# Three queues reordered: centring the first batch's weights later in each step, and a new order of DVE's and ACT's work behind attention

## Chip, cores and metric

The kernel runs on one core of one Trainium2 chip. The metric is the device time of one launch in microseconds (us). PE is TensorE (matmuls and transposes), DVE is VectorE, ACT is ScalarE, POOL is GpSimd, and SP is SyncE, which here only issues transfers. Each engine has a queue of its own, works it off in order, and waits at semaphores.

## What is computed

Eight sequences of 256 tokens, width 256, go through a gated attention layer and a gated mixture of experts:

```python
x = x + tanh(g_xattn) * attention(layernorm(x), ctx)     # self (256 keys) and cross (64 keys)
x = x + tanh(g_ffn) * moe(layernorm(x))                  # 8 experts, 2 for each token, one shared expert

# attention: ln -> fp8 rounding -> q, qx (16 heads), k, v (8 groups), each q and k head with a
# layernorm of its own over its 128 columns; kx, vx from ctx in full precision; softmax; p @ v;
# both outputs divided by a smoothing vector, rounded to fp8, and projected by wproj
```

## The kernel before

**Attention** runs in steps n = 0 to 63: step n = 8b + g belongs to batch b and head group g. A step is a software pipeline. In step n, PE projects q, k, v of group n, transposes the normalised heads of group n-1, scores group n-1, multiplies the probabilities of group n-4 by v, and projects group n-5 out. The first batch is written out step by step (`tick(0, g)`); the other seven run in a loop. Steps 64 to 68 drain the pipeline and already hold work of the experts.

**What each engine does in a step, in its queue's order.** ACT: `copy_q` (the projected q to SBUF, L884), `square_q`, in the first batch `scale(k)`, then squares and copies of k, `high_p`, `key_maps` (L913), `exp_cross`, `high_v`, and last `exp_self` (L924). DVE: `read_q` twice (L1236), the sums of squares (`squares_q`, which waits for ACT's `square_q` of the same step), variances (L1250), `low_p` (L1208), the row maxima of the scores (L1203, which wait for PE, which waits for `key_maps`), `low_v` (L1219), `copy_x` (L1230), reciprocals, and the next batch's front: statistics in steps 0 and 1, `front_scale` in step 2, a clip in step 3. POOL: the roots (L1693), the product that normalises q (L1760), k (L1767, waits for `copy_x`), `probx` (L1737) and `prob` (L1744), and in steps 0 and 1 the next batch's layernorm (L1697, L1700).

**The weights of the first batch.** The projections' weights come in eight pieces, k = 0 to 7, one for each group, through two staging buffers. For each piece DVE sums the heads (`sum_heads`, L1150), turns the sums to means (`head_means`) and subtracts them from the scaled weights (`centre`, eight instructions, L1166); ACT rounds the result to f16 (`high(k)`, L832); and POOL takes the rest (`prepare(k)` on POOL, `w_lo`, L1727). Piece 0 is made before step 0, pieces 1 and 2 in step 0, and piece k in step k-2 after that. PE may project step k when `w_lo` of piece k is there. SP loads piece k into its buffer when `w_lo` of piece k-2 is done. The transposing transfer `flip(0)`, which brings the probabilities of group 0 to where PE multiplies them by v in step 4, stands in SP's queue behind the wait for `w_lo` of piece 5.

In DVE's step the parts of one piece lie apart: `sum_heads` between the two `read_q`, `centre` in the middle, ahead of the maxima. On ACT, `high(k)` stands ahead of `exp_self`.

**Behind attention.** The experts' weights are split into an f16 high part (ACT, `ffn_high(u)`, L837) and a low part (DVE, `ffn_low(u)`, L1180), in units u = 0 to 4: u = 0 is the shared expert, the others hold two experts each. The shared expert runs for six pieces m = 0 to 5 in the first half: PE `shared_up(m)`, ACT `shared_silu(m)`, DVE `shared_mul(m)` (L1584), ACT `shared_high(m)` (L850), POOL `shared_low(m)` (L1810), PE `shared_down(m)` (L659 to L661). DVE adds its results to x in `finish(q)` (L1595). Routing is DVE's: `ranks`, `count_tiles`, `plan_tiles`, `read_table`, `read_tokens` (the row addresses, `f_idx`), `slots` and `mix_weights`. POOL then gathers the experts' rows with indirect transfers (`fetch_z(j)`, L1820), behind `tail_low` of the last batch (L1721), which waits for ACT's `tail_high` (L818). The experts' loop of 39 tiles begins on PE with `expert_up(0)`, which waits for all five `ffn_low`; PE's `turn_z(1)` waits for `finish(3)`; DVE's `expert_mul(0)` follows `mix_weights`.

Of the kernel before, what the change touches and what calls it, by code (L numbers as in the profile page):

```python
# [16 lines left out]
B, S, SC, H = 8, 256, 64, 256  # L17
# [57 lines left out]
def build(nc, x, wallT, wpT, w13T, w2e, s1T, s3T, s2, gateT, ctxT, vecs, scal, ident, rconst, rtri, out):  # L75
    ctx = ExitStack()
    with ctx:
# [725 lines left out]
        def _(act):  # L803
# [11 lines left out]
            def tail_high(tb):  # L815
                done(act, ta_z, tb)
                act.wait_ge(zr_read, tb * 32 + 16)
                nc.scalar.activation(zr[:, :, 0, :], zf[:, :, :], ACT.Copy).then_inc(ta_hi, 1)  # L818
# [33 lines left out]
            def tick(b, g):  # L852
# [162 lines left out]
                    front_scale(b + 1)  # L1015
                if g == TAIL_G and live(b - 1, B):
                    tail_high(b - 1)
                for k in preps[-1:]:
                    high(k)
                for h in range(HPG):  # L1020
                    if live(n0 - 1): exp_self(n0 - 1, par(1), h)

            act.wait_ge(ld_vec, 48)
            nc.scalar.activation(gates[:, 0:2], scl[:, S_GX:S_GF + 1], ACT.Tanh).then_inc(tanh_done, 1)
# [44 lines left out]
            ffn_high(3)  # L1069
            shared_silu(3)  # L1070
            ffn_high(4)
            shared_high(3)
            shared_silu(4)
            tail_high(B - 1)
            shared_high(4)
            shared_silu(5)
            shared_high(5)
# [13 lines left out]
        def _(dve):  # L1091
# [98 lines left out]
            def tick(b, g):  # L1190
# [91 lines left out]
                if isinstance(n0, int) and n0 >= STEPS:  # L1282
                    if g == 0:
                        for k in (1, 0): read_q(n0 - 1, par(1), k)
                        whole_out(n0 - 5, par(5))
                        maxima(n0 - 2, par(2), 2)
                        low_p(n0 - 3, par(3))
                        low_px(n0 - 3, par(3))
                        for k in range(2): maxima(n0 - 1, par(1), k)
                        sums(n0 - 2, par(2))  # L1290
                        read_logits(0, 0, NE, A1)
                        done(dve, mm_kT, STEPS - 1)
                        best(0, 0, NE, 0)
                        maxima(n0 - 1, par(1), 2)
                        best(0, 0, NE, 1)
                        members(0, NE)
                        sums(n0 - 1, par(1))
                        low_p(n0 - 2, par(2))
                        low_px(n0 - 2, par(2))
                    if g == 1:  # L1300
                        ranks(0)
                        count_tiles(0)
                        whole_out(n0 - 5, par(5))
                        low_p(n0 - 2, par(2))
                        low_px(n0 - 2, par(2))
                        ffn_low(0)
                    if g == 2:
                        whole_out(n0 - 5, par(5))
                        for t in range(4): marks(t)
                        ffn_low(1)  # L1310
                        shared_mul(0)
                    if g == 3:
                        whole_out(n0 - 5, par(5))
                        for t in range(4, 8): marks(t)
                        shared_mul(1)
                        whole_out(n0 - 4, par(4))
                        for t in range(8, NE): marks(t)
                        shared_mul(2)
                    return
# [2 lines left out]
                    prepare(k)  # L1322
                if tail and g == LAGS: residual(b - 1)
                if live(n0 - 1): read_q(n0 - 1, par(1), 1)
                if preps and n0 > 0: sum_heads(preps[-1])
                if live(n0 - 1): read_q(n0 - 1, par(1), 0)
                if live(n0): squares_q(n0, par(0))
                if live(n0): low_vx(n0)
# [3 lines left out]
                if live(n0 - 2): maxima(n0 - 2, par(2), 2)  # L1332
                if live(n0 - 5): round_out(n0 - 5, par(5))
                if live(n0): variances_k(n0, par(0))
                if preps and n0 == 0:
                    low_v(n0)
                    copy_x(n0, par(0))
                    sum_heads(preps[-1])
                if preps: head_means(preps[-1])
                for c in range(HC if preps else 0): centre(preps[-1], c)  # L1340
                if live(n0 - 3): low_p(n0 - 3, par(3))
                if live(n0 - 3): low_px(n0 - 3, par(3))
                if between and g == G - 1:
                    done(dve, mm_q1, n0)
                    front_round(b + 1, 0)
                if live(n0 - 1): maxima(n0 - 1, par(1), 0)
                if live(n0) and not (preps and n0 == 0):
                    low_v(n0)
                    copy_x(n0, par(0))
                if live(n0 - 1): maxima(n0 - 1, par(1), 1)  # L1350
                if live(n0 - 2): sums(n0 - 2, par(2))
                if between:
                    if isinstance(n0, int) and n0 == 0:
                        dve.wait_ge(ld_x, 16)
                    if g == 0: front1(b + 1)
                    if g == 1: front2_stats(b + 1)
                    if g == FRONT_G: front_scale(b + 1)
                    if g == FRONT_G + 1: front_clip(b + 1)
                    if g == G - 1:
                        done(dve, mm_kv, n0)  # L1360
                        front_round(b + 1, 2)
                if tail:
                    if g == LAGS: tail1(b - 1)

# [271 lines left out]
            tail1(B - 1)  # L1636
            plan_tiles(0)
            read_table(0)
            ffn_low(2)
            read_tokens(0)  # L1640
            for q in range(2): finish(q)
            shared_mul(3)
            ffn_low(3)
            shared_mul(4)
            ffn_low(4)
            shared_mul(5)
            slots(0)
            for q in range(2, 4): finish(q)
            mix_weights(0, 0, NE)
# [244 lines left out]
```

## Time and profile before

| | |
|---|---|
| median of 3 runs | 967.53 us (966.03 to 969.52) |
| the profiled execution's own time | 960.57 us |
| its span in the trace | 958.8 us |
| busy, share of the span | PE 86%, DVE 83%, ACT 79%, POOL 76% |
| first batch's steps 1 to 6 | about 48 to 135 us |
| loop of batches 1 to 7 | to about 720 us |
| first tile of the experts' loop | at 796.66 us |

A row of the timeline gives start and duration in us, engine, line, operation, output <- inputs with their shapes, and in brackets the engine's idle time before it and who ended it.

### The profile page before, as it was taken

Reading aid. Unit: us, or ns where it says so; the run is one execution under the profiler, and the core shown is the slowest. Engines: PE = TensorE matmul, PEld = TensorE weight load, DVE = VectorE, ACT = ScalarE, POOL = GpSimd, SP = SyncE. Lnnn points to the kernel's source line nnn. Section 1 sums busy time; section 2 is a strip of 40 time slices with the busy share of each in tenths; the row PEclk is TensorE's granted clock in tenths of the full one; section 3 lists DMA queues with packets and bytes.
Section 4 is the critical chain, followed back from the end, with each engine's and each line's share of the span. In section 5 each row is a group of like instructions: output and inputs, shape, how many; then the busy total and the mean of one; then the engine's idle time right before and its main releaser. Section 6 shows DMA issues by size and latency. Waiting matters only on the chain.

```text
span 958.8 us, 21329 instructions
## 1 busy us (share of the span) xinstructions
PE 825.3 (86%) x6498; PEld 638.5 (67%) x6498; DVE 799.0 (83%) x1857; ACT 756.2 (79%) x2392; POOL 725.2 (76%) x570
## 2 busy tenths in 40 slices
PE   0467699999999999999999999999995858888396
PEld 0345478788778778878777877877874436666254
DVE  7999889998998998999898899989888986743148
ACT  3367799999999999999999999999997433444132
POOL 4398689899889989988998998899896145444633
PEclk9777999999999999999999999999999799999689
DMA  9521433235234324324324333333337524556433
GB/s 247 130 88 45 100 66 74 57 60 101 55 58 85 70 55 82 77 55 82 77 55 78 59 77 72 64 77 75 61 85 173 147 88 111 131 140 145 125 120 112
DMA packets 213837, 87.64 MB, mean 91 GB/s; under 512 B 190080, under 2 KB 207456, under 8 KB 213792
## 3 DMA queue, kind: packets, MB, share of 16 engines
q1 hardware_dynamic: 205936, 74.76, 34.9%
q0 software_dynamic: 7856, 12.33, 5.9%
q8 instruction: 23, 0.38, 0.2%
q14 instruction: 22, 0.18, 0.1%
HBM read 31.88 MB, written 10.22 MB: 44 GB/s over the span
## 4 chain that ended last, share of the span: by engine, by line
PE 35%; POOL 23%; DVE 15%; issue 14%; ACT 7%; DMA 3%; another core or an unknown queue 2%; DVEq 0%; POOLq 0%; SPq 0%; ACTq 0%
POOL rstd L1693 8%; POOL raw L1760 5%; PE A L432 5%; PE A L433 5%; PE T L498 4%; PE S L527 3%; POOL prob L1744 3%; PE S L515 2%; DVE stage L1166 2%; DVE ss L1241 2%; POOL z L1700 2%; DMA psrc<-w_lo 2%; POOL z L1697 2%; ACT zq L811 2%
## 5 line engine op out<-in xcount | busy, mean ns | idle before, releaser
L1693 POOL TENSOR_TENSOR rstd<-var,mhalf 128x8 f32<-128x8 f32 (+1 forms) x128 | 190.3, 1503 | 54.3 <-DVE var L1250 53.9
L432 PE MATMUL A<-w_hi,xq 128*128 128x256 f16 (+1 forms) x1024 | 190.2, 251 | 36.6 <-DVE v_lo L1219 20.7
L433 PE MATMUL A<-w_lo,xq 128*128 128x256 f16 (+1 forms) x1024 | 190.4, 252 | 0.0
L1236 DVE TENSOR_SCALAR qT<-T,qmap 128x512 f32<-128x512 f32 x128 | 103.5, 810 | 56.8 <-PE T L498 56.5
L527 PE MATMUL S<-kT,qT 128*128 128x256 f32 x512 | 139.1, 395 | 5.6 <-ACT kT L913 4.9
L432 PEld LDWEIGHTS A<-w_hi,xq 128*128 128x128 f16 x1024 | 102.0, 100 | 49.0 <-issue 32.2
L924 ACT ACTIVATE prob<-S,nmx 128x256 f32<-128x256 f32 x256 | 122.0, 503 | 7.1 <-DVE nmx L1203 5.2
L527 PEld LDWEIGHTS S<-kT,qT 128*128 128x128 f32 x512 | 92.8, 191 | 45.8 <-ACT kT L913 27.9
L1760 POOL TENSOR_TENSOR raw<-raw,rstd 128x1024 f32<-128x1024 f32 x64 | 121.2, 1894 | 0.0
L1744 POOL TENSOR_TENSOR prob<-prob,rl 128x1024 f32<-128x1024 f32 x64 | 121.0, 1891 | 0.0
L1203 DVE TENSOR_REDUCE nmx<-S 128x2 f32<-128x512 f32 (+1 forms) x192 | 113.5, 591 | 4.1 <-PE S L527 3.4
L433 PEld LDWEIGHTS A<-w_lo,xq 128*128 128x128 f16 x1024 | 102.1, 100 | 8.2
L498 PE MATMUL T<-idt,raw 128*128 128x128 f32 x512 | 82.1, 285 | 8.4 <-POOL raw L1760 7.4
L1820 POOL DMA_INDIRECT w_lo<-zd,w_lo x46 | 45.2, 982 | 54.1 <-PE VB L747 26.7
L884 ACT ACTIVATE raw<-A 128x512 f32<-128x512 f32 x128 | 81.5, 637 | 4.5 <-PE A L433 4.5
L932 ACT ACTIVATE probx<-S,nmx 128x64 f32<-128x64 f32 x256 | 78.0, 338 | 3.7 <-DVE nmx L1203 3.6
L1208 DVE SCALAR_TENSOR_TENSOR psrc<-prob,psrc 128x1024 f16<-128x1024 f32 x64 | 78.3, 1224 | 1.6 <-ACT psrc L948 1.5
L1241 DVE TENSOR_REDUCE ss<-sq 128x8 f32<-128x1024 f32 x64 | 77.4, 1209 | 0.0
L877 ACT ACTIVATE sq<-A 128x512 f32<-128x512 f32 x128 | 72.4, 639 | 4.0 <-PE A L433 4.0
L498 PEld LDWEIGHTS T<-idt,raw 128*128 128x128 f32 x512 | 61.4, 146 | 18.1 <-POOL raw L1760 15.7
L557 PE MATMUL JB<-wp,yb 128*128 128x256 f16 x512 | 67.2, 275 | 6.3 <-DVE yb L1271 6.3
L948 ACT ACTIVATE psrc<-prob 128x1024 f16<-128x1024 f32 x64 | 67.9, 1061 | 1.4 <-POOL prob L1744 1.4
(257 smaller groups left out, 2434.1 us busy)
## 6 DMA issues: line engine op xcount, KB each, us to landing
stage<-wallT SPq DMA_DIRECT2D x8, 1024.0 KB, 5.1
yd<-pT SPq DMA_DIRECT2D x46, 128.0 KB
wp<-wpT POOLq DMA_DIRECT2D x1, 2048.0 KB, 31.0
zd<-zr SPq DMA_DIRECT2D x8, 256.0 KB, 2.4
out<-xs SPq DMA_DIRECT2D x8, 256.0 KB
xs<-x SPq DMA_DIRECT2D x1, 1792.0 KB, 21.0
raw<-w13T SPq DMA_DIRECT2D x2, 704.0 KB, 4.6
pT<-psrc SPq DMA_TRANSPOSE x64, 4.9
```

The costliest lines, as they stand in the source:

```text
L432: nc.tensor.matmul(o, l, w_hi[:, c, col:col + n], start=(c == 0), stop=False)
L433: last = nc.tensor.matmul(o, l, w_lo[:, c, col:col + n], start=False, stop=(c == HC - 1))
L498: last = nc.tensor.transpose(o[:, h * S + t * P:h * S + (t + 1) * P], raw[:, p, UQ + t * 2 * HPG + k * HPG + h, :], idt[:, :])
L527: last = nc.tensor.matmul(o[:, t * S:(t + 1) * S], qT[:, p, 0, h, t * P:(t + 1) * P], kT[:, p, 0:S], start=True, stop=True)
L884: last = nc.scalar.activation(raw[:, p, u, :], o, ACT.Copy)
L924: last = nc.scalar.activation(prob[:, p, :, j, :], o[:, t * S:(t + 1) * S].rearrange("p (k s) -> p k s", s=P), ACT.Exp, bias=nmx[:, p, j:j ...
L1203: nc.vector.tensor_reduce(nmx[:, p, j:j + rows], o[:, 0:rows * w].rearrange("p (r w) -> p r w", w=w), AX.X, ALU.max, negate=True).then_inc ...
L1236: nc.vector.tensor_scalar(qT[:, p, k, :, :].rearrange("p h s -> p (h s)"), o[:, :], qmap[:, 2 * k:2 * k + 1], qmap[:, 2 * k + 1:2 * k + 2] ...
L1241: nc.vector.tensor_reduce(ss[:, p, 0:UK], sq[:, p, 0:UK, :], AX.X, ALU.add).then_inc(d_ssq, 1)
L1693: return nc.gpsimd.tensor_tensor(dst, src, mhalf[:, 0:n], ALU.pow)
L1744: nc.gpsimd.tensor_tensor(prob[:, p, :, :, :], prob[:, p, :, :, :], rl[:, p, 0:PJ].rearrange("p (o j i) -> p o j i", o=1, i=1).to_broadcas ...
L1760: nc.gpsimd.tensor_tensor(raw[:, p, 0:UK, :], raw[:, p, 0:UK, :], rstd[:, p, 0:UK].rearrange("p (u o) -> p u o", o=1).to_broadcast([P, UK, ...
```

## The change

It has two parts. In the first batch, DVE makes a whole piece of weights (`prepare(k)`: sums, means, centring) at the end of its step, behind the maxima and the next batch's front; the special order of step 0 goes; and on ACT `high(k)` stands behind `exp_self`. Behind attention, DVE runs `ranks` and `count_tiles` behind `ffn_low(0)`; `finish(0)` and `finish(1)`, `read_tokens(0)`, `shared_mul(3)` and `shared_mul(4)` ahead of `ffn_low(2)`, and `shared_mul(5)` ahead of `ffn_low(3)`; and ACT runs `tail_high` of the last batch ahead of `shared_high(3)`. No instruction is added, removed or altered, and no buffer or wait is another.

```diff
 # ACT, end of a step
+                for h in range(HPG):
+                    if live(n0 - 1): exp_self(n0 - 1, par(1), h)
                 for k in preps[-1:]:
                     high(k)
-                for h in range(HPG):
-                    if live(n0 - 1): exp_self(n0 - 1, par(1), h)
...
 # ACT, behind step 68
             ffn_high(4)
+            tail_high(B - 1)
             shared_high(3)
             shared_silu(4)
-            tail_high(B - 1)
...
 # DVE, step 65
                     if g == 1:
-                        ranks(0)
-                        count_tiles(0)
                         whole_out(n0 - 5, par(5))
                         low_p(n0 - 2, par(2))
                         low_px(n0 - 2, par(2))
                         ffn_low(0)
+                        ranks(0)
+                        count_tiles(0)
...
 # DVE, a step of the first batch
                 if live(n0 - 1): read_q(n0 - 1, par(1), 1)
-                if preps and n0 > 0: sum_heads(preps[-1])
                 if live(n0 - 1): read_q(n0 - 1, par(1), 0)
...
-                if preps and n0 == 0:
-                    low_v(n0)
-                    copy_x(n0, par(0))
-                    sum_heads(preps[-1])
-                if preps: head_means(preps[-1])
-                for c in range(HC if preps else 0): centre(preps[-1], c)
...
                 if live(n0 - 1): maxima(n0 - 1, par(1), 0)
-                if live(n0) and not (preps and n0 == 0):
-                    low_v(n0)
-                    copy_x(n0, par(0))
+                if live(n0): low_v(n0)
+                if live(n0): copy_x(n0, par(0))
                 if live(n0 - 1): maxima(n0 - 1, par(1), 1)
...
                         front_round(b + 1, 2)
+                for k in preps[-1:]:
+                    prepare(k)
...
 # DVE, behind step 68
             read_table(0)
+            for q in range(2): finish(q)
+            read_tokens(0)
+            shared_mul(3)
+            shared_mul(4)
             ffn_low(2)
-            read_tokens(0)
-            for q in range(2): finish(q)
-            shared_mul(3)
+            shared_mul(5)
             ffn_low(3)
-            shared_mul(4)
             ffn_low(4)
-            shared_mul(5)
             slots(0)
```

## Rows read from the trace of the kernel before

**Rows 1.** Stretches: busy us of PE, PEld, DVE, ACT, POOL (instructions), granted clock, DMA.

```profile
40.00:60.00 20.00, 12.34 (x66) 8.56 (x65) 19.53 (x45) 10.32 (x25) 15.61 (x13) 0.67 0.28 101
...
220.00:300.00 80.00, 78.23 (x626) 62.92 (x624) 72.74 (x164) 78.61 (x264) 72.24 (x57) 1.00 0.36 70
```

**Rows 2.** Timeline of ACT in the first batch: `copy_q` of steps 1, 2, 5, 7.

```profile
47.56 0.58 ACT L884 ACTIVATE raw<-A 128x512 f32<-128x512 f32 x1
...
59.98 0.61 ACT L884 ACTIVATE raw<-A 128x512 f32<-128x512 f32 x1
...
71.77 1.91 ACT L832 ACTIVATE w_hi<-stage 128x2048 f16<-128x2048 f32 x1 [1.03 <-DVE stage L1166]
...
108.99 0.64 ACT L884 ACTIVATE raw<-A 128x512 f32<-128x512 f32 x1
...
113.88 0.89 ACT L913 ACTIVATE kT<-T,vec 128x256 f32<-128x256 f32 x2
...
135.30 0.61 ACT L884 ACTIVATE raw<-A 128x512 f32<-128x512 f32 x1
```

**Rows 3.** Timeline of DVE in the first batch.

```profile
60.92 1.80 DVE L1150 TENSOR_REDUCE msum<-stage 128x6 f32<-128x768 f32 x2
...
67.41 1.14 DVE L1166 SCALAR_TENSOR_TENSOR stage<-stage,vec,msum 128x256 f32<-128x256 f32 x3
...
68.67 2.81 DVE L1166 SCALAR_TENSOR_TENSOR stage<-stage,vec,msum 128x256 f32<-128x256 f32 x3
...
105.02 0.69 DVE L1203 TENSOR_REDUCE nmx<-S 128x2 f32<-128x512 f32 x1 [2.39 <-PE S L527]
```

**Rows 4.** Timeline of POOL in the first batch.

```profile
51.78 0.69 POOL L1693 TENSOR_TENSOR rs<-ve,mhalf 128x2 f32<-128x2 f32 x1
...
61.78 1.04 POOL L1700 TENSOR_TENSOR z<-z,rs 128x512 f32<-128x512 f32 x1
...
66.97 2.49 POOL L1693 TENSOR_TENSOR rstd<-var,mhalf 128x8 f32<-128x8 f32 x2
69.44 1.89 POOL L1760 TENSOR_TENSOR raw<-raw,rstd 128x1024 f32<-128x1024 f32 x1
73.00 0.83 POOL L1767 TENSOR_TENSOR raw<-raw,rstd 128x384 f32<-128x384 f32 x1 [1.68 <-DVE raw L1230]
...
74.36 1.90 POOL L1744 TENSOR_TENSOR prob<-prob,rl 128x1024 f32<-128x1024 f32 x1
```

**Rows 5.** The chain that ended last: start, us, what.

```profile
92.04 4.05 POOL w_lo L1727
...
96.11 5.01 DMA pT<-psrc
...
131.53 0.97 PE S L527 x4
```

**Rows 6.** Timeline of DVE behind attention.

```profile
756.03 0.43 DVE L1266 TENSOR_SCALAR yb<-yb 128x1024 f16<-128x1024 bf16 x1 [0.59 <-ACT yb L957]
...
775.31 2.75 DVE L1180 SCALAR_TENSOR_TENSOR w_lo<-sq,w_hi 128x1408 f16<-128x1408 f32 x2
...
789.26 0.69 DVE L1584 SCALAR_TENSOR_TENSOR zq<-S,qT 96x512 f32<-96x512 f32 x1 [2.43 <-POOL w_hi L1810]
789.87 1.79 DVE L1570 TENSOR_TENSOR ctx_hi<-ctx_hi,ctx_lo 128x192 f32<-128x192 f32 x1
...
795.52 0.88 DVE L1595 SCALAR_TENSOR_TENSOR xs<-VB,gates,xs 128x256 f32<-128x256 f32 x2 [1.51 <-issue]
```

**Rows 7.** Timeline of POOL behind attention.

```profile
782.28 1.94 POOL L1721 TENSOR_TENSOR zr<-z,zr 128x512 f16<-128x512 f32 x1 [9.20 <-ACT zr L818]
784.38 2.30 POOL L1820 DMA_INDIRECT w_lo<-zd,w_lo  x1 [0.17 <-issue]
```

**Rows 8.** Timeline of ACT behind attention.

```profile
780.57 0.63 ACT L850 ACTIVATE w_hi<-zq 128x512 f16<-128x512 f32 x1 [6.01 <-DVE zq L1584]
```

**Rows 9.** Timeline of PE: the first matmul of `expert_up(0)`.

```profile
796.66 0.32 PE L424 MATMUL S<-w_hi,psrc 128*128 x1 [0.60 <-issue]
```

## The prediction

> **What bounds the kernel now.** I read the stretches first. In the loop of batches 1 to 7 ACT is busy for 78.6 of 80 us and PE for 78.2 [rows 1]; nothing of the change lies there, and what the first batch loses or gains simply shifts the loop. In the first batch the picture is another: from 40 to 60 us DVE is busy for 19.5 of 20 us, ACT for 10.3 and PE for 12.3 [rows 1]. There DVE sets the pace. Then I read the timelines of ACT, DVE and POOL side by side, with `copy_q` as the mark of a step: step 1 takes 12.4 us (47.56 to 59.98), steps 2 to 4 take 49.0, steps 5 and 6 take 26.3 [rows 2]. The loop's step is about 10.2: 264 ACT instructions in 80 us, some 33.6 of them to a step [rows 1].
>
> Two things are to be seen in DVE's rows. Centring c = 0 takes 1.14 us, the same three instructions for c = 1 take 2.81 [rows 3], and the added 1.67 us lie inside POOL's product of 69.44 to 71.33 [rows 4]. So DVE is held while POOL runs a large product, and this recurs in each step from 1 to 5. And DVE hardly waits for anybody: `sum_heads` and `centre` fill what would be waits for ACT's squares and for PE's scores. Only step 4 has a real one, 2.39 us for the scores [rows 3], whose cause is the chain `w_lo` of piece 5 until 96.09, then the 5.01 us transposing transfer [rows 5].
>
> Behind attention I followed DVE to the first tile of the experts at 796.66 [rows 9]. It waits 0.59 us at 756.03, 2.43 at 789.26 and 1.51 at 795.52 [rows 6]; the second is POOL's `shared_low(3)`, which is late because POOL stands idle for 9.20 us until ACT's `tail_high` and then still has 1.94 us of `tail_low` and 2.30 us of the first gather ahead of it [rows 7].
>
> **First part: a loop through two engines.** Nothing is removed, so the cost is one of order. Let C be the time at which `centre` ends. In the new order ACT's `high(k)` waits for C, and everything of ACT's next step is queued behind it; `copy_q`, `key_maps`, then PE's scores, then DVE's maxima, and only behind these DVE's next `sum_heads` and `centre`. From C to the next C this is:
>
> - `high` 1.91 [rows 2];
> - from the start of `copy_q` to the end of `key_maps` 5.8 (108.99 to 114.77) [rows 2]; ACT hardly idles in it;
> - from there to the end of the second pair of scores 2.6 and one maximum of 0.7: 3.3. The 2.6 is `key_maps` ending 1.6 before the scores of 131.53, and their 0.97 [rows 5];
> - a reciprocal and `sum_heads` 1.9 [rows 3];
> - centring twice 1.26 (67.41 to 68.67), 2.5 [rows 3], and `head_means` with the latencies 0.3.
>
> That is 15.7 us, against 15 now for steps that DVE fills by itself. In the new order DVE waits about 2 us for ACT's squares (they end 3.5 us after C, two `read_q` of 0.7 fill 1.5) and again ahead of the maxima, where centring stood as cover. To this comes what is particular to a step:
>
> - Step 0: centring of piece 2 must wait for POOL's two products of q and k. `high(2)` ends 0.6 later: `copy_q(1)` at 48.1.
> - Step 1: DVE gets to centring at about 59.7, when POOL is in the middle of its step. POOL's queue from 48.2: `w_lo` 4.05 [rows 5], the front 2.9 (root 0.69, two products of 1.04 and a gap), roots 2.49, q 1.89, k 0.83, the front again 2.9 [rows 4]: until 63.3. Three centring instructions pass between, five (1.5 us) come after: C at 64.8, `copy_q(2)` at 66.8. The step is 18.7 against 12.4.
> - Step 2: no `high_p` yet (less 1.25), but `front_scale` behind ACT's half of it (plus 1.9), and the end of `prob` (plus 0.2): 16.5. Step 3: the clip, 0.9 more: 16.6.
> - Step 4: `high(5)` 1.9, `w_lo` 4.1, and only then `flip(0)`, 5.0 [rows 5], 3.9 from its landing at 101.12 to the maxima at 105.02 [rows 3], 2.0 for both maxima, 1.9 for the sums, 0.7 until `prob` is done, 2.5 centring: 22.1 with latencies; one new `scale_out` on ACT 0.85: 23.0. Now, with centring in the middle of step 3, `w_lo` of piece 5 is done that much earlier against the scores that PE has queued behind `flip(0)`. Steps 2 to 4: 56.1 against 49.0.
> - Step 5: 15.7, plus 0.85 for `scale_out` ahead of `copy_q` on ACT, plus 1.4 because `prob` (1.90) [rows 4] holds centring of piece 7: 17.9. Step 6 has no piece: 10.2. Together 28.1 against 26.3.
>
> The sum is 0.6 + 6.3 + 7.1 + 1.8 = **15.8 us longer**. The move takes DVE past no queue of its own DMAs; SP's loads wait for `w_lo` of two pieces before and come a step ahead of need even so (piece 7: issued near 108, wanted by ACT at 125). The bounds: if POOL's products hold DVE nowhere, steps 0, 1, 4 and 5 lose 0.6, 2.5, 0.7 and 1.4 less: +10. If each of some eight handovers a step costs 0.1 more, in five steps, +20. I take 14.5, a little below the sum, nearer to the lower bound: the scores of steps 4 and 5 have no `scale_out` of the other output behind them yet, and PE may hand over each half early.
>
> DVE is held by POOL as the Trainium skill says in "SBUF — State Buffer", Who interferes with whom: a DVE instruction with two SBUF inputs waits for a GpSimd instruction that reads SBUF, for the whole of it, while a reduction never does. The trace agrees (2.81 against 1.14; `sum_heads` is 1.80 even beside `w_lo`). By that rule the move should pay, as most of centring leaves POOL's product of q; that is the first rival.
>
> **Second part: behind attention.** `ffn_low(0)` ends 3.0 earlier, since `ranks` and `count_tiles` now stand behind it; these delay nobody (their readers, `marks(0)` and `plan_tiles`, come when they came). PE's `shared_up(0)` starts 3 us earlier and the 0.59 us wait at 756.03 [rows 6] goes; DVE is full otherwise: gain 0.6. After `read_table`, which ends at 775.3 (I leave the 0.6 out until the end), DVE does: `finish` twice 1.6, `read_tokens` 0.3, `shared_mul(3)` 0.6, until 777.9. `shared_mul(4)` waits for ACT's `shared_high(3)` and silu: 1.2, then 0.6. Three `ffn_low` of 2.7 [rows 6], one more `shared_mul` 0.6, `slots` 1.2 where nothing holds it (its first instruction is 1.79 now, with `shared_low` beside it [rows 6]), `finish` twice 1.6: 791.3. ACT's `tail_high` runs at about 774.6 in its 6.01 us of idleness [rows 8], so POOL's `tail_low`, gathers and `shared_low(3)` come some 6 to 7 us earlier, which removes the 2.43 and the 1.51, but the three `shared_low` of 1.2 now run beside `ffn_low` and may hold DVE for up to 3.5. I take 1.5: 792.8. Now `finish(3)` ends at 797.1. With the 0.6 the experts' loop starts **4.9 earlier**; bounds 3 and 7. PE's last `shared_down` and the logits are ready by 789 and do not bind; `expert_up(0)` waits for `ffn_low(4)` at about 790. Should the loop be paced by its gathers, these are early by as much.
>
> **The sum.** 14.5 − 4.9 = +9.6, taken as +9 for the profiled execution's 960.57: 969.6. The median shown is 967.53, 7 above that execution, so about **976.5 us**.
>
> **Rivals.**
> - *POOL's hold is what costs* (the gain side). If DVE alone sets the first batch and the waits through ACT are hidden, removing 1.67 in five steps takes off 8.4, and the tail 4.9 with it: 954. More likely half of it, as steps 1 and 4 must still lose: −1 and −4.9, 961.5. For it: DVE at 98% busy [rows 1]. Against: `squares_q` needs ACT, and ACT stands behind `high(k)`. It decides if ACT's path from C to `key_maps` were under some 5 us instead of 7.7. Chance 0.14 for faster by over 0.3% (2.9 us), which is about what a measurement of this kernel can tell from no change.
> - *The two parts cancel*: first part +5 to +7 since PE and ACT hand over early, tail −5: 965 to 970. Chance 0.10.
> - *The tail gives nothing*: the experts' loop is paced by its gathers and its transposing transfers, and POOL's `shared_low` holds `ffn_low` fully: +14.5 and 0, 982. For it: the collisions; against: the three waits are real. Chance 0.08.
> - The forecast, +4 to +13 (971.5 to 981): 0.68.
>
> Slower by over 0.3%: 0.76; same 0.10; faster 0.14. The range 965 to 983 leaves out the gain side and the far end of the third rival.
>
> **What would show it.** Right: in DVE's timeline of 65 to 140 us, idle time ahead of L1241 (released by ACT's squares) and of L1203 (released by PE), where now there is none; ACT idle ahead of L832 until centring; `copy_q` of steps 2, 5 and 7 near 67, 123 and 150 us; the first tile of the experts' loop 4 to 6 us nearer to the end of attention. Wrong: L1166 at 1.14 us throughout and steps of 14 us or less; or `copy_q(2)` before 63. The forecast fails above all if steps 1 and 4, which carry 10 of the 15.8 us (18.7 against 12.4, 23.0 against some 19), are mistaken.

## The result, and the profile after

| | before | after |
|---|---|---|
| median on one chip (4 runs of each) | 966.78 us (965.39 to 969.52) | 988.1 us (986.92 to 988.6) |
| ratio, 95% interval | | 1.0232 (1.0188 to 1.0276) |
| profiled execution, its span | 960.57, 958.8 us | 986.92, 985.1 us |
| mean granted clock of TensorE | 0.953 | 0.936 |
| `copy_q` of steps 1 to 7 start at | 47.56, 59.98, 75.39, 90.06, 108.99, 124.11, 135.30 | 47.72, 65.82, 83.66, 102.10, 125.78, 144.89, 156.48 |
| DVE's first `read_q` of step 65 | 723.08 us | 744.45 us |
| first `expert_mul` | 798.66 us | 817.38 us |

The change costs 21.3 us, outside the predicted 965 to 983. Behind the loop of batches 1 to 7, which keeps its length, `read_q` of step 65 is a good mark: it is 21.4 us later. The first batch alone carries the whole loss. From there to the first `expert_mul`, 75.6 us have become 72.9, but that lead is gone at the end (+21.3 in the medians).

Stretches of the kernel after (columns as in [rows 1]):

```profile
40.00:60.00 20.00, 11.82 (x69) 8.26 (x68) 15.66 (x34) 8.73 (x23) 15.38 (x12) 0.75 0.27 99
60.00:80.00 20.00, 12.78 (x80) 9.86 (x77) 14.70 (x31) 11.65 (x35) 14.66 (x10) 0.74 0.15 52
80.00:100.00 20.00, 12.46 (x65) 9.79 (x65) 14.62 (x34) 11.29 (x33) 12.19 (x7) 0.66 0.16 54
100.00:120.00 20.00, 12.76 (x69) 9.10 (x69) 9.82 (x19) 12.13 (x35) 11.31 (x7) 0.66 0.51 119
```

DVE, which bounded the first batch with 19.5 of 20 us [rows 1], is busy for 15.7, 14.7, 14.6 and 9.8. No engine is full. The granted clock, the last column but two, is 0.74 and 0.66 in the two stretches from 60 to 100 us. A clock of 1.00 is TensorE's full 2.4 GHz, 0.50 its lower level of 1.2 GHz; values between are a mix of the two.

Step 3 on DVE in the kernel after, from one centring to the next:

```profile
80.40 1.14 DVE L1166 SCALAR_TENSOR_TENSOR stage<-stage,vec,msum 128x256 f32<-128x256 f32 x3
...
85.24 1.22 DVE L1241 TENSOR_REDUCE ss<-sq 128x8 f32<-128x1024 f32 x1 [2.06 <-ACT sq L877]
87.22 0.28 DVE L1224 SCALAR_TENSOR_TENSOR vx_lo<-T,vx_hi 64x128 f16<-64x128 f32 x1 [0.76 <-ACT vx_hi L895]
...
92.14 0.69 DVE L1203 TENSOR_REDUCE nmx<-S 128x2 f32<-128x512 f32 x1 [1.70 <-PE S L527]
...
95.12 1.81 DVE L1150 TENSOR_REDUCE msum<-stage 128x6 f32<-128x768 f32 x2
96.96 0.59 DVE L1157 TENSOR_TENSOR msum<-msum,smean 128x12 f32<-128x12 f32 x1
97.59 1.14 DVE L1166 SCALAR_TENSOR_TENSOR stage<-stage,vec,msum 128x256 f32<-128x256 f32 x3
98.65 0.28 DVE L1166 SCALAR_TENSOR_TENSOR stage<-stage,msum 128x128 f32<-128x128 f32 x1
98.85 1.14 DVE L1166 SCALAR_TENSOR_TENSOR stage<-stage,vec,msum 128x256 f32<-128x256 f32 x3
```

Both of the waits that the prediction named are there: 2.06 us for ACT's squares, 1.70 for PE's scores. Centring is held by nobody in this step (1.14 and 1.14 against the 1.14 and 2.81 of [rows 3]), and still the step takes 18.4 us. What is left of the hold has moved to `head_means` (L1157): it takes 0.59 us here, 0.88 and 1.32 in steps 4 and 5, each time until POOL's `prob` ends, and 0.17 in step 2, where `prob` was over. The same step on ACT:

```profile
81.84 1.91 ACT L832 ACTIVATE w_hi<-stage 128x2048 f16<-128x2048 f32 x1 [4.76 <-DVE stage L1166]
83.66 0.58 ACT L884 ACTIVATE raw<-A 128x512 f32<-128x512 f32 x1
...
89.11 0.86 ACT L913 ACTIVATE kT<-T,vec 128x256 f32<-128x256 f32 x2 [0.44 <-PE T L507]
```

Each engine waits for the other once a turn: ACT 4.76 us for centring, DVE for what ACT then sets off. PE in the same step:

```profile
86.53 1.91 PE L515 MATMUL S<-kT,qT 128*128 128x64 f32 x8
90.03 3.78 PE L527 MATMUL S<-kT,qT 128*128 128x256 f32 x8 [0.95 <-ACT kT L913]
```

Both rows lie in time at the lower clock (granted 0.50 from 86.5 to 88.4 us and from 90.0 to 93.8). In the kernel before the same sixteen matmuls took 1.06 us at 79.01 (granted 1.00) and 2.84 at 82.10 (0.78).

Waits of DVE that begin with step 4 of the kernel after:

```profile
115.83 0.69 DVE L1203 TENSOR_REDUCE nmx<-S 128x2 f32<-128x512 f32 x1 [6.94 <-PE S L527]
...
127.16 0.81 DVE L1236 TENSOR_SCALAR qT<-T,qmap 128x512 f32<-128x512 f32 x1 [3.28 <-PE T L498]
...
146.27 0.81 DVE L1236 TENSOR_SCALAR qT<-T,qmap 128x512 f32<-128x512 f32 x1 [3.28 <-PE T L498]
```

The first is `flip(0)`, 2.39 us in [rows 3]; its chain in the kernel after (start, us, what) is:

```profile
102.28 4.09 POOL w_lo L1721
...
106.38 5.62 DMA pT<-psrc
```

The 3.28, twice, is one that the prediction does not have. Behind it on PE:

```profile
126.03 1.09 PE L498 MATMUL T<-idt,raw 128*128 128x128 f32 x4 [6.63 <-ACT yb L957]
```

and on ACT:

```profile
123.25 1.91 ACT L832 ACTIVATE w_hi<-stage 128x2048 f16<-128x2048 f32 x1 [4.38 <-DVE stage L1166]
125.06 0.82 ACT L957 ACTIVATE yb<-T,rsm 128x256 bf16<-128x256 f32 x2
```

PE transposes the second half of q into the buffer T1, which the cross attention's output (`pT` times `vx`, made in step 4) still fills. ACT empties it with `scale_out(·, 1)` (L957), the first work of its next step, and that now stands behind `high(k)`, which waits for DVE's centring, while DVE then waits for PE's transposes.

### The profile page after: what moved, and what is told of

It is laid out like the page before. It is cut to its first block, busy times and chain, and to the rows that moved or that the text cites. A ratio compares the mean times of both kernels' runs of the same rounds, so it can differ in the third digit from the quotient of the medians.

```text
span 985.1 us, 21329 instructions
## 1 busy us (share of the span) xinstructions
PE 834.3 (85%) x6498; PEld 645.1 (65%) x6498; DVE 793.4 (81%) x1857; ACT 756.7 (77%) x2392; POOL 728.2 (74%) x570
## 4 chain that ended last, share of the span: by engine, by line
PE 37%; POOL 23%; DVE 15%; issue 14%; ACT 7%; DMA 2%; another core or an unknown queue 1%; POOLq 0%; DVEq 0%; SPq 0%; ACTq 0%
POOL rstd L1687 8%; POOL raw L1754 5%; PE A L432 4%; PE T L498 4%; PE A L433 4%; PE S L527 4%; POOL prob L1738 3%; PE S L515 3%; DVE stage L1166 2%; PE S L424 2%; DVE ss L1241 2%; POOL z L1694 2%; ACT zq L811 2%; POOL z L1691 2%; PE S L425 1%
## 5 line engine op out<-in xcount | busy, mean ns | idle before, releaser
L924 ACT ACTIVATE prob<-S,nmx 128x256 f32<-128x256 f32 x256 | 122.2, 505 | 11.8 <-DVE nmx L1203 10.0
L1814 POOL DMA_INDIRECT w_lo<-zd,w_lo x46 | 47.7, 1036 | 56.0 <-PE VB L747 29.3
L515 PE MATMUL S<-kT,qT 128*128 128x64 f32 x512 | 71.1, 284 | 1.1 <-ACT prob L924 1.1
```

The source lines that it names most:

```text
L515: last = nc.tensor.matmul(S0[:, k * SC:(k + 1) * SC], qT[:, p, 1, h, t * P:(t + 1) * P], kT[:, p, S:KT], start=True, stop=True)
L924: last = nc.scalar.activation(prob[:, p, :, j, :], o[:, t * S:(t + 1) * S].rearrange("p (k s) -> p k s", s=P), ACT.Exp, bias=nmx[:, p, j:j ...
```

## Experiments

Ratios are to the kernel before on the same chip. "Drain" is the start of `read_q` of step 65 (723.08 before). Some kernels hold unused matmuls, whose result nothing reads; the expectations also call them fillers or unused transpositions, and the early `flip(0)` of e3 and e4 the second flip. A first remark on what one trace can carry: of seven other kernels whose code is the old one up to step 3, five put `copy_q(4)` within 0.4 us of 90.06 and two (e13, e15) at 86.63 and 88.53. In the new order step 1 takes 18.1 us in four traces (after, e3, e9, e14) and 19.2 in three (e1, e5, e7), on the same code. So a difference of 2 to 3 us between single traces is weak; a wait named in the trace, or a ratio with its interval, is not.

**e1 and e2: each part alone.** e1 has the hunks of the diff above for the first batch and ACT's end of a step, e2 those behind attention.

> Only the first batch's part of the change: weights prepared at the end of DVE's steps, high(k) behind exp_self; everything behind attention as before. Theory A (the first batch holds the whole loss, through the loop over two engines): 20 to 22 us slower than before, copy_q of step 7 near 156.5 us as in the changed kernel. Rival B (each part costs): 15 us or less.

e1: 984.81 us, ratio 1.0218 (1.0180 to 1.0256), drain 745.56.

> Only the part behind attention, the first batch as before. My prediction's term: 4.9 us faster (3 to 7). Rival from the changed kernel's trace, where the first tile came 2.7 us nearer to attention's end but the loop behind it lost it again: within 1.5 us of before. Third: slower by 2 to 5 us.

e2: 963.42 us, ratio 1.0000 (0.9980 to 1.0019), drain 722.78, first `expert_mul` 73.0 us behind the drain (before 75.6). The parts add up: the first is the loss, and the second is worth nothing that this interval can show.

**e3 and e4: is `flip(0)` the cost of step 4?** In the change (e3) and in the kernel before (e4) it is issued ahead of SP's wait for `w_lo`:

```diff
+                if k == G - 1:
+                    flip(0)
                 if k >= 2:
                     sp.wait_ge(w_lo_done, k - 1)
-                if k == G - 1:
-                    flip(0)
```

> The changed kernel with SP's flip(0) issued ahead of the wait for w_lo of piece 5. If step 4's 6.94 us wait for scores is the chain high(5), w_lo(5), flip(0), it goes: 6 to 7 us faster than the changed kernel, so about 14 to 15 us slower than before. Rival (something else would end the wait just after): 2 us or less of gain.

> The kernel before with SP's flip(0) ahead of the wait for w_lo of piece 5. In before, the scores of step 4 waited 2.39 us, and ACT sat idle for 4.70 us for the same transfer: 2 to 4 us faster than before if so; nothing, if DVE's own work fills the step.

e3: 981.63 us, 1.0183 (1.0149 to 1.0218), drain 740.73, step 4 19.7 instead of 23.7. e4: 962.18 us, 0.9967 (0.9948 to 0.9986), step 4 15.8 instead of 18.9. The queue of the flip costs in both kernels, some 4 us in the new one, where 6 to 7 were expected: with the flip out of the way DVE's 6.94 us wait in step 4 becomes one of 2.94, still for the scores.

**e5: the missed edge.** e1, with `scale_out(·, 1)` of the next step issued by ACT ahead of `high(k)`:

```diff
+                early = isinstance(n0, int) and 1 <= n0 <= 6
-                if live(n0 - 5): scale_out(n0 - 5, par(5), 1, group(5))
+                if live(n0 - 5) and not early: scale_out(n0 - 5, par(5), 1, group(5))
...
                 for h in range(HPG):
                     if live(n0 - 1): exp_self(n0 - 1, par(1), h)
+                if isinstance(n0, int) and n0 <= 5 and live(n0 - 4): scale_out(n0 - 4, par(4), 1, group(4))
                 for k in preps[-1:]:
                     high(k)
```

> The first batch's part alone, with ACT's scale_out of the cross output (the one that opens the next step) moved ahead of high(k) in steps 1 to 5. In the changed kernel the second transposing of q in steps 5 and 6 waited for it: DVE 3.28 us each time, PE 6.33. Theory A (this missed edge is part of the cost): these waits shrink by about 1.5 each and the kernel is 2 to 3 us faster than the part alone. Rival: the squares and key_maps end last anyway, under 1 us.

986.04 us, 1.0255 (1.0209 to 1.0301). In the trace both waits of 3.28 us are gone, steps 5 and 6 take 17.7 and 11.8 (e1 18.2 and 12.0), and the drain stands at 743.62, 1.9 earlier. The times do not show it: the interval overlaps that of e1. In the place of the 3.28 us of step 5 DVE now has two other waits:

```profile
128.03 1.22 DVE L1243 TENSOR_REDUCE ss<-sq 128x8 f32<-128x1024 f32 x1 [2.06 <-ACT sq L877]
...
134.92 0.69 DVE L1205 TENSOR_REDUCE nmx<-S 128x2 f32<-128x512 f32 x1 [1.36 <-PE S L527]
```

So the edge exists, but the late transposes covered waits of the loop that were there anyhow: in the trace e5 gains 0.5 and 0.2 us in steps 5 and 6 (and 0.9 in step 4, ACT's own time for `scale_out`), and the 2 to 3 us that were expected did not come.

**e6: ACT's half of the move undone.** e1 with `high(k)` ahead of `exp_self`, as in the kernel before.

```diff
+                for k in preps[-1:]:
+                    high(k)
                 for h in range(HPG):
                     if live(n0 - 1): exp_self(n0 - 1, par(1), h)
-                for k in preps[-1:]:
-                    high(k)
```

> The first batch's part on DVE only: preparation at the end of its step, but ACT's high(k) ahead of exp_self as before. If ACT's whole next step hangs on centring, exp_self (1.8 us) now comes behind it as well: 5 steps x 1.8, 8 to 10 us slower than the first batch's part alone. Rival: DVE's and POOL's side ends last, then about equal.

995.9 us, 1.0354 (1.0310 to 1.0399), drain 755.01. Once DVE centres at the end, ACT's new order saves 9.5 us in the drain (13 by the ratios): the exponentials would otherwise stand behind the same wait. That ACT's next step hangs on centring is shown by this.

**e12: ACT's half alone.** The kernel before with `high(k)` behind `exp_self`, DVE as it was (the two ACT hunks of the diff above).

> The kernel before with only ACT's part of the first batch's change: exp_self ahead of high(k). There the maxima come behind centring, so high(k) would be ready first and now waits for them and for exp_self: w_lo and flip(0) come 2 to 3 us later in each step. Expected: slower than before by 1 to 4 us, far from the 21 us of both together; rival: equal to before, DVE's own work filling the step.

964.77 us, 1.0035 (1.0010 to 1.0060), drain 726.83. By itself ACT's order costs a little: `high(k)` of step 2 starts at 74.44 instead of 71.77 [rows 2], as the exponentials ahead of it wait for the maxima. The bulk of e1's 2.2% comes from DVE's order.

**e7, e9, e14: the clock, and all losses taken away in turn.** e7 is e1 with 14 unused matmuls a step in PE's idle time; e9 is e5 with 12; e14 is e9 with the flip of e3.

```diff
+                if isinstance(n0, int) and 1 <= n0 <= 6:
+                    done(pe, a_e0, n0 - 2)
+                    for _ in range(12):
+                        nc.tensor.matmul(S1[:, :], w_hi[:, 0, 0:P], w_hi[:, 0, 0:512], start=True, stop=True)
                 if live(n0): project_x(n0)
```

> The first batch's part alone plus 14 matmuls a step (128 x 512, f16) in steps 1 to 6 on PE, into a bank that is free, where PE idles ahead of the ctx projection; they add work and compute nothing. Theory A: PE's idleness brought the granted clock down (0.66 to 0.75 in 60 to 120 us) and scores at the lower clock take 1.9 and 3.8 us instead of 1.1 and 2.1, so with the clock kept up the kernel gets 4 to 8 us faster than the part alone. Rival (the waits alone): equal, or slower by the filler that runs into the path.

> The kernel with scale_out early, plus 12 filler matmuls a step in steps 1 to 6 ahead of the ctx projection (extra work, no result used). In the earlier filler run steps 5 and 6 had the fillers on the path, behind ACT's late scale_out, and lost there what steps 2 to 4 won (1.6, 0.6 and 1.0 us). Here the second transposing no longer waits, so the fillers lie in idle time in every step: copy_q of step 7 comes 4 to 6 us earlier than with scale_out early alone (155.96), if the granted clock carries that much. Rival: 1 us or less.

> The first batch's part of the change alone, with the scaling by 1 of each step issued ahead of the high weights, unused transpositions to hold the clock, and the second flip's eviction moved forward (what it gave in the kernel before: 2 us; in the new loop: 5 us). Theory: the late scaling, the clock and the flip are three separate losses beside the loop between ScalarE and VectorE; with all three taken away the start of the main part comes 4 to 5 us ahead of its place with the first two (740.7 us), near 736, and the ratio is 1.009 to 1.013: some 13 us of loss stay, which is the loop itself. Rival: the flip is hidden once the clock is held, and nothing is gained on 740.7: ratio 1.015 to 1.017.

| | us | ratio | drain | steps 1 to 6 |
|---|---|---|---|---|
| e1 | 984.81 | 1.0218 (1.0180 to 1.0256) | 745.56 | 19.2, 18.1, 18.5, 23.9, 18.2, 12.0 |
| e7 | 989.24 | 1.0304 (1.0259 to 1.0349) | 749.47 | 19.2, 16.5, 17.8, 22.9, 22.8, 14.5 |
| e9 | 977.27 | 1.0160 (1.0119 to 1.0201) | 740.68 | 18.1, 17.8, 18.5, 22.8, 17.9, 10.3 |
| e14 | 969.64 | 1.0082 (1.0058 to 1.0106) | 732.68 | 18.1, 16.5, 18.5, 16.7, 17.1, 10.3 |

e7 failed as a version and told two things: with the clock at 1.00 within step 2 that step took 16.5 us, which is the predicted number; and in steps 5 and 6 the unused matmuls, which follow the late transposes, came on the path ahead of the ctx projection (5.68 us for 14 of them at 125.36), so that DVE waited 4.65 and 3.51 us for ACT's copy of it. With `scale_out` early (e9) that collision is gone; `copy_q` of step 7 comes at 153.00, 3.0 us ahead of e5, where 4 to 6 were expected. Step 2 stayed at 17.8 in e9: its mean clock was 0.90, but its scores still ran at the lower one (1.92 us at 68.37, against 1.06 at 67.98 in e14). e14 then gained 8.0 us on e9 in the drain where the theory said 4 to 5, and 0.78% in the ratio; 1.3 of the 8.0 lie in step 2, where the two kernels have the same code. Stretches of e14:

```profile
80.00:100.00 20.00, 14.94 (x81) 11.01 (x81) 14.62 (x32) 12.24 (x34) 12.19 (x7) 0.74 0.32 86
100.00:120.00 20.00, 14.20 (x111) 9.81 (x108) 14.49 (x28) 15.84 (x44) 13.92 (x8) 1.00 0.35 87
120.00:140.00 20.00, 15.66 (x110) 10.91 (x110) 17.08 (x37) 15.27 (x47) 15.12 (x9) 1.00 0.18 34
```

With the flip early, step 4 falls from 22.8 to 16.7 and the clock is 1.00 from 100 us (in e9 0.83). Ahead of that, in step 3, it was 0.72 in spite of the unused matmuls, and the scores took as long as in the kernel after:

```profile
88.79 3.78 PE L527 MATMUL S<-kT,qT 128*128 128x256 f32 x8 [0.95 <-ACT kT L917]
```

And two of its DVE rows of step 5:

```profile
119.10 1.22 DVE L1247 TENSOR_REDUCE ss<-sq 128x8 f32<-128x1024 f32 x1 [2.05 <-ACT sq L881]
...
128.52 2.73 DVE L1172 SCALAR_TENSOR_TENSOR stage<-stage,vec,msum 128x256 f32<-128x256 f32 x3
```

The wait for the squares remains, and `prob` holds centring of piece 7, as the prediction's step 5 has it. With flip and scaling out of the way, what remains in the steps that had the full clock is the loop of the two engines: 16.5, 16.7 and 17.1 us for steps 2, 4 and 5. The ratio of 1.0082 also holds step 3 at 18.5 with a clock of 0.72. The least disturbed form of the change is thus still some 8 us slower than the kernel before, and 11 slower than that kernel with the same early flip (e4). No run gives the old order of the first batch the same unused matmuls; its clock is 0.72 to 0.91 in steps 1 to 5, so at an equal clock the loop may cost more than these 11 us.

**e8: half a move.** The kernel before with ACT's new order and the early flip, and with DVE centring one half ahead of the maxima and one behind.

```diff
+                split = bool(preps) and n0 > 0
...
-                for c in range(HC if preps else 0): centre(preps[-1], c)
+                for c in range((1 if split else HC) if preps else 0): centre(preps[-1], c)
+                if split:
+                    maxima(n0 - 1, par(1), 0)
+                    low_v(n0)
+                    copy_x(n0, par(0))
+                    maxima(n0 - 1, par(1), 1)
+                    centre(preps[-1], 1)
...
-                if live(n0 - 1): maxima(n0 - 1, par(1), 0)
-                if live(n0) and not (preps and n0 == 0):
+                if live(n0 - 1) and not split: maxima(n0 - 1, par(1), 0)
+                if live(n0) and not preps:
                     low_v(n0)
                     copy_x(n0, par(0))
-                if live(n0 - 1): maxima(n0 - 1, par(1), 1)
+                if live(n0 - 1) and not split: maxima(n0 - 1, par(1), 1)
```

> The kernel before with flip(0) ahead of the wait (3 us faster by itself), and centring split: chunk 0 where it was, then both maxima, low_v and copy_x, which read PSUM, in the time of POOL's product, then chunk 1; high(k) behind exp_self. Theory: chunk 1 takes 1.1 instead of 2.8 us in steps 1 to 5, so another 4 to 8 us: 7 to 11 us faster than before. Rival: the maxima come too early and wait for the scores as long as POOL held chunk 1: 2 to 4 us faster than before, by the flip alone.

966.4 us, 1.0050 (1.0020 to 1.0080), drain 727.53. Row of ACT in it:

```profile
89.86 0.47 ACT L924 ACTIVATE prob<-S,nmx 128x256 f32<-128x256 f32 x1 [4.60 <-DVE psrc L1208]
```

Both the theory (7 to 11 us faster) and its rival (2 to 4) missed: against e4 it loses 0.8%. Its steps 3, 4 and 5 take 17.8, 17.9 and 17.1 us, in e4 14.8, 15.8 and 16.0. The row shows one more edge that was overlooked: ACT's `exp_self` may not write `prob` before DVE's `low_p` of an earlier group has read it (4.60 us in step 3, 4.70 and 4.01 in the next two), `low_p` now stands behind both halves of centring and the maxima, and `high(k)` stands behind `exp_self`. ACT's order costs 0.35% by itself (e12), so e8 does not tell what the split alone costs with `low_p` kept early.

**e10, e11, e13, e15, e16: where the second part's lead goes.** In e2, at the start of the experts' loop, PE's matmuls run at half the clock (granted 0.50 from 790 to 800 us). First the kernel e2, then its stretch:

```profile
793.43 0.47 PE L424 MATMUL S<-w_hi,psrc 128*128 x1 [0.57 <-issue]
```

```profile
795.00:805.00 10.00, 8.28 (x59) 5.44 (x58) 6.18 (x28) 4.18 (x12) 3.85 (x5) 0.74 0.38 92
```

and that of the kernel before:

```profile
795.00:805.00 10.00, 6.96 (x76) 4.96 (x74) 6.56 (x26) 2.99 (x9) 5.69 (x6) 1.00 0.45 109
```

The same matmul took 0.32 us before [rows 9]. Just ahead of this the kernel before is no better off: 0.66 from 785 to 795 us, 0.58 in e2. A second spell near 0.50 in e2, from 824 to 827 us, has no counterpart before. The lead of 2.6 us at the first `expert_mul` row is 1.4 at the 11th and 0.2 at the 16th. So unused matmuls were put ahead of the shared expert's last pieces and of tiles 10 and 11: into the new order (e10; with the early flip e11, and again e16), and as a control into the old one (e13; with the early flip e15). PE's wait for `d_x1` moves ahead with them.

```diff
+            done(pe, d_x1, B - 1)
-            for m in range(3, M0): shared_down(m)
+            for m in range(3, M0):
+                for _ in range((8, 9, 9)[m - 3]):
+                    nc.tensor.matmul(JB[:, 0:SHARED], s1_hi[:, 0, 0:P], s1_hi[:, 0, 0:SHARED], start=True, stop=True)
+                shared_down(m)
             pe.wait_ge(zr_read, 16 + 32 * B)
-            done(pe, d_x1, B - 1)
...
+                if j in (10, 11):
+                    done(pe, e_y, j - DL - 2)
+                    for _ in range((6, 10)[j - 10]):
+                        nc.tensor.matmul((A0, A1)[(j - DL) % 2][:, 0:SHARED], s1_hi[:, 0, 0:P], s1_hi[:, 0, 0:SHARED], start=True, stop=True)
                 if j >= DL: expert_down(j - DL)
```

> The part behind attention alone plus filler matmuls on PE (extra work, no result used): 8, 9 and 9 ahead of shared_down(3), (4), (5), and 6 and 10 ahead of the tenth and eleventh tile's expert_down, where PE idled and the granted clock then fell to 0.5. Theory A (the clock took back the 2.9 us that the new order wins): the second tile comes at 75.2 us behind the drain's first read_q instead of 76.3, tile 14 at about 106 instead of 108.4, and the kernel is 1 to 3 us faster than before. Rival B (later tiles wait for gathers and transposing transfers anyhow): the early tiles come sooner, but within 1 us of before in the end.

> The same with flip(0) ahead of the wait for w_lo of piece 5: the flip's 3.2 us and whatever the run without it shows, added: 3 to 6 us faster than before.

> The kernel before with its old order behind attention and the same unused transpositions by TensorE (their result is read by nothing) that the filler version of the new tail has. Theory: in the old tail the granted clock was 1.00 already, so the fillers have nothing to restore: ratio 0.999 to 1.003, and the gain of the new tail with fillers (0.9953) is the new order with its clock given back. Rival: the fillers alone carry the gain, whatever the order: ratio 0.995 to 0.997.

> The kernel before with the second flip early and the unused transpositions, and the old order behind attention. Theory (the new order carries part of the gain): ratio 0.995 to 0.998, and 2 us or more slower than the next kernel, which differs from it in the order behind attention alone. Rival (the unused work and the flip carry all of it, the order nothing): the same as the next kernel within 1 us.

> The second flip early, the unused transpositions and the new order behind attention, on the same chip as the kernel above. Measured once at 0.9933 (0.991 to 0.9956). Theory: 0.991 to 0.995 again, and 2 us or more below the kernel with the old order. Rival: within 1 us of it.

| | order | flip | unused work | us | ratio | first and last (46th) row of `expert_mul` in the trace, behind the drain |
|---|---|---|---|---|---|---|
| before | old | late | none | | 1 | 75.6, 198.7 |
| e2 | new | late | none | 963.42 | 1.0000 (0.9980 to 1.0019) | 73.0, 201.8 |
| e10 | new | late | yes | 957.74 | 0.9953 (0.9934 to 0.9972) | 72.6, 197.1 |
| e13 | old | late | yes | 958.37 | 0.9973 (0.9953 to 0.9992) | 78.2, 198.9 |
| e4 | old | early | none | 962.18 | 0.9967 (0.9948 to 0.9986) | 75.7, 205.0 |
| e15 | old | early | yes | 960.09 | 0.9973 (0.9953 to 0.9993) | 77.0, 198.4 |
| e11 | new | early | yes | 955.24 | 0.9933 (0.9910 to 0.9956) | 71.0, 192.6 |
| e16 | new | early | yes | 956.68 | 0.9924 (0.9894 to 0.9954) | 72.7, 195.1 |

The last rows cannot be compared so closely: with the same code behind attention they lie at 198.7 (before), 196.9 (e14), 198.1 (e1), 201.7 (e12) and 205.0 (e4, whose profiled execution was the slowest of its twelve). What counts is the ratio. With the unused matmuls the new order is 3.4 us faster than the old one on the same chip (e15, e16). Of the clock the traces say less: the unused matmuls raise it ahead of the loop (785 to 795 us: 0.58 in e2, 0.99 in e10 and e16), but from 795 to 805 it is 0.67 in e10 and 0.84 in e16, against 0.74 in e2. So that the whole gain is clock given back is not shown. The control is not quite fair to the old order: there `finish` is near the end of the path, and the unused matmuls stand ahead of `shared_down`. DVE in e15:

```profile
794.58 0.88 DVE L1602 SCALAR_TENSOR_TENSOR xs<-VB,gates,xs 128x256 f32<-128x256 f32 x2 [4.36 <-PE T L661]
```

In e13 and e15 the first `expert_mul` comes 2.6 and 1.3 us later than in before and in e4. Against the old order without them (e4) e11 and e16 gain 0.34% and 0.43%, with intervals that just overlap, and e10 gains 0.47% on the kernel before, more than the 1 to 3 us that were expected. e13 missed what the theory expected of it (0.999 to 1.003), whose premise that the old tail's clock was 1.00 already does not hold from 785 to 795 us (0.66): the unused matmuls alone may carry part of the gain. Its trace differs from before's in steps 2 and 3 too, where the code is the same, so it settles little by itself. e11 and e16 are one kernel, measured on two chips, and the best version found: it beats both kernels, by 0.7% and 2.9%.

## Why the prediction was wrong in size

It had the sign and the mechanism (slower, a loop through two engines), and missed by 11.7 us: forecast +9.6, taken as +9; measured +21.3. Two terms of its sum failed: the first batch (15.8 us, taken as 14.5) measured 21.2, mainly because the rows that priced the loop came from steps with a higher clock; and the 4.9 us to be won behind attention came to nothing at the end. In its own terms:

| step | predicted | after | e14 |
|---|---|---|---|
| `copy_q(1)` later by | 0.6 | 0.2 | 0.2 |
| step 1 | 18.7 | 18.1 | 18.1 |
| step 2 | 16.5 | 17.8 | 16.5 |
| step 3 | 16.6 | 18.4 | 18.5 |
| step 4 | 23.0 | 23.7 | 16.7 |
| step 5 | 17.9 | 19.1 | 17.1 |
| step 6 | 10.2 | 11.6 | 10.3 |
| first batch in all | +15.8, taken 14.5 | +21.2 | |
| behind attention | -4.9 | -2.7 at the first tile, 0 at the end | |

**Right.** The loop itself with its two waits (about 2 us for the squares were forecast, 2.06 measured), and the step that was feared most: 18.1 for step 1. POOL's hold on centring went in steps 2 to 5 (the 1.14 and 1.14 above), and where POOL's products still stood beside centring it stayed (2.73 in e14). This is as the Trainium skill has it in "SBUF — State Buffer", Who interferes with whom, for a DVE instruction with two SBUF inputs. The rival that took this hold for the price was wrong: DVE has the time back as waits.

**Mis-sized: a loop priced with rows of the old clock.** The 5.8 us for `copy_q` to `key_maps` and the 3.3 from there to the second maximum are rows of steps with a granted clock of 0.91 and 0.97 (steps 5 and 6 of the kernel before). In step 3 of the kernel after, at 0.69, they are 6.3 (83.66 to 89.97, with 0.44 of waiting for PE's transposes) and 4.6 (to 94.54): these two make up the 1.8 us by which the step is over its forecast. In step 2 of e14, at 1.00, the second is 3.3 again (70.39 to 73.73). The credit of 1.25 us for the missing `high_p` in step 2 was void for the same reason: ACT had the time and waited for PE (1.42 us at 71.02). With a clock of 1.00 step 2 is 16.5, as forecast (e7, e14), and step 6, at 10.3 in e9 and e14, is close to its 10.2. Steps 2, 3 and 6 are together 4.5 us over their forecasts, of the 5.4 by which the first batch is over its 15.8. Step 3 had the full clock in no trace (17.8 us at 0.90 in e7), and step 1 does not depend on it (18.1 at 0.75, 0.91 and 1.00). `head_means`, for which with all latencies 0.3 was set, took 0.59 us in step 3 as POOL's `prob` held it.

**Missed: one edge.** The prediction charged `scale_out` in steps 4 and 5 as 0.85 us of ACT's time. It is also what frees PE's buffer for the second half of q; behind `high(k)` it turned into two waits of 3.28 us. The queue behind a new wait was listed for ACT's own products, and not for the buffers that it frees. By e5 the edge is no large part of the miss: 0.7 us in the two steps. The prediction's reading that DVE had only one real wait, in step 4, also passed over 1.19 us at 90.91 and 2.00 at 124.56, both for PE's transposes of q.

**Right in place: step 4.** Its 23.0 was near (23.7). The chain of `w_lo` and `flip(0)` costs 4.0 us of it without unused matmuls (e3) and 6.1 with them (e9 against e14), where the mean clock of the step also rises, from 0.85 to 1.00.

**Wrong direction: the cut.** The 15.8 was lowered to 14.5 by judgement. The bound of +20 (a tenth of a us for each handover) was nearer, though for a reason that the runs do not bear out. The range's end of 983 holds +20 only together with the whole 4.9 us behind attention; with nothing from there it is 987.5.

**Mis-sized: behind attention.** The waits of 2.43 and 1.51 us went, and `tail_high` ran early. But the lead is 2.7 us instead of 4.9, for two terms. The wait of 0.59 us, booked as a gain of 0.6, went from its place, but one of 1.54 for ACT's `scale_out` appeared a step later; why was not traced. And of the three `ffn_low`, priced at 2.7 each and 1.5 for collisions, 9.6 in all, 10.9 passed: 4.06, 3.10 and 3.70 (before 2.75, 2.75 and 3.11). The first is worth 0.6 that did not come and 1.0 on top, the second 1.3; some 0.7 came back in the smaller work around them and in a shorter wait ahead of `expert_mul(0)`, and 2.2 are missing. Both on DVE in the kernel after:

```profile
784.60 0.43 DVE L1266 TENSOR_SCALAR yb<-yb 128x1024 f16<-128x1024 bf16 x1 [1.54 <-ACT yb L957]
...
802.35 4.06 DVE L1180 SCALAR_TENSOR_TENSOR w_lo<-sq,w_hi 128x1408 f16<-128x1408 f32 x2
```

POOL beside it:

```profile
801.65 0.95 POOL L1814 DMA_INDIRECT w_lo<-zd,w_lo  x1 [0.30 <-issue]
...
803.95 2.17 POOL L1814 DMA_INDIRECT w_lo<-zd,w_lo  x1 [0.16 <-issue]
806.13 1.30 POOL L1804 TENSOR_TENSOR w_hi<-zq,w_hi 128x512 f16<-128x512 f32 x1
807.58 2.16 POOL L1814 DMA_INDIRECT w_lo<-zd,w_lo  x1 [0.15 <-issue]
```

The collisions cost both sides: the gathers that stand beside an `ffn_low` take 2.17 us instead of 0.95. What was left of the gain went in the first 16 rows of `expert_mul`, in whose time TensorE ran at half clock twice (e2); that this is the cause is made likely by e10, and not shown. Of the rivals, "the tail gives nothing" named the outcome at a chance of 0.08, and with its 982 was still 6 us short, as it kept the 14.5.

**Open.** What the late `scale_out` is worth alone (its trace says 2 us in the drain, its time nothing), what the loop costs against an old order with the same clock, and how much of the 3 to 4 us of the new order behind attention is the order and how much PE's fuller start.

## What to carry to other kernels

Small work that fills an engine's waits looks like load (DVE at 98%); before it is moved, price the waits that it covers, since two engines that alternate take the sum of their turns. When a new wait is put on an engine, list the buffers that the work behind it frees for third engines, beside what it produces. And price a loop that will be longer with matmuls at both clock levels: here the rows of the old kernel gave only the lower bound.

## What was not expected of the hardware

- The granted clock was low where PE's work came in short turns: 0.67 to 0.83 in the stretches from 40 to 80 us before, 0.66 from 80 to 120 us after. With a dozen unused matmuls a step and the early flip it was 1.00 from 100 us on (e14), but still 0.74 from 80 to 100. The Trainium skill says in "TensorE: Matmul & The Clock Gate", Part 1, that the slow level is the default and activity lifts it; these rows agree.
- An indirect transfer's issue on POOL took 2.17 us instead of 0.95 beside a DVE instruction with two SBUF inputs, three times in the kernel after; the first gather before, 2.30 us beside the third of the `ffn_low` behind `read_table` [rows 7], fits. In "SBUF — State Buffer", Who interferes with whom, the Trainium skill infers that such an instruction does not slow the making of descriptors; these rows speak against that for this form, though no run here isolates the pair.
- Old code can differ by 3 us between two traces (`copy_q(4)` at 90.06 and 86.63). The medians of the kernel before on the five chips of the experiments differ as much, 961.03 to 964.53 us, which is why each ratio is to the kernel before on the same chip.
